# Layer 2 heads reordered in pairs of levels, layer 1 weight folds moved into the layer 0 head norm

## The reference, cut to what matters

```python
q = causal_depthwise_conv(x @ Wq, qcw, qcb); k = ...; v = ...   # 4 taps, then silu
def step(St, inp):
    q_, k_, v_, a_, b_ = inp
    sk = einsum('bhij,bhj->bhi', St, k_)
    err = sk - v_
    Sn = a_[..., None, None] * St - b_[..., None, None] * err[..., None] * k_[..., None, :]
    return Sn, einsum('bhij,bhj->bhi', Sn, q_)
o = layernorm(o) * ln_w + ln_b;  o = o * sigmoid(x @ Wg);  return o @ Wo
```

## Time and profile before

| what | value |
|---|---|
| runs | 2279.02 us median of 3 (2278.3 to 2285.44) |
| profiled execution | 2279.3 us |
| its span, first to last instruction | 2277.6 us |
| mean granted clock of TensorE | 0.909 |
| TensorE busy (matmuls) | 1916.4 us, 84% |
| VectorE, ScalarE, GpSimd busy | 1228.4, 836.2, 461.2 us |

### The profile page before, as it was taken

The page is one execution under the profiler, slowest core; times in us unless marked ns, Lnnn a source line. Parts: engine busy times, 40 slices in busy tenths (PEclk is TensorE's granted clock), DMA queues, the critical chain, the costliest instruction groups (busy, mean ns, idle before and its releaser), DMA issues. The chain is left out here.

```text
span 2277.6 us, 52273 instructions
## 1 busy us (share of the span) xinstructions
PE 1916.4 (84%) x21233; PEld 1321.6 (58%) x21233; DVE 1228.4 (54%) x3235; ACT 836.2 (37%) x1973; POOL 461.2 (20%) x536
## 2 busy tenths in 40 slices
PE   7993779997999995765999999999899797679569
PEld 3443644565777562553666766666667684456456
DVE  7957542343663346644566666666666326642641
ACT  1112321221652222223576666666666203220120
POOL 0012410330000332641221221122111003720200
PEclk9996999896999998787999999999999798789779
DMA  5000000621500516751010001001000127830000
GB/s 181 0 1 1 1 1 14 210 94 55 205 1 3 186 38 210 241 208 40 21 41 21 21 22 40 21 21 37 25 22 21 52 46 215 258 149 15 3 2 20
DMA packets 55330, 157.37 MB, mean 69 GB/s; under 512 B 12899, under 2 KB 29881, under 8 KB 50822
## 3 DMA queue, kind: packets, MB, share of 16 engines
q1 hardware_dynamic: 45206, 128.84, 16.9%
q0 software_dynamic: 9888, 25.20, 3.3%
HBM read 115.36 MB, written 40.48 MB: 68 GB/s over the span
## 5 line engine op out<-in xcount | busy, mean ns | idle before, releaser
L2268 PE MATMUL l_heads_ps_p<-xnT,l2a_w 128*128 128x512 f32 x512 | 257.0, 628 | 8.2 <-DMA l2a_w<-in_l_w_heads 8.2
L2668 DVE SCALAR_TENSOR_TENSOR l_heads_taps<-l_heads_padded,l_heads_conv,l_heads_taps 128x1024 f32<-128x1024 f32 x144 | 183.8, 1286 | 8.2 <-ACT l_heads_taps L2494 7.5
L2268 PEld LDWEIGHTS l_heads_ps_p<-xnT,l2a_w 128*128 128x128 f32 x512 | 89.5, 194 | 80.4 <-issue 64.2
L2843 POOL TENSOR_TENSOR l_heads_e<-l2a_table,l_heads_row 128x512 f32<-128x512 f32 x32 | 33.3, 1042 | 390.6 <-DVE l_heads_first L2679 385.3
L198 PE MATMUL norm_turn<-zeros,ident 128*128 128x512 f32 x120 | 67.1, 716 | 53.5 <-PEq L60 53.5
L189 ACT ACT_TABLE_LOAD x10 | 12.8, 1283 | 207.2 <-PEq L60 207.2
L198 PEld LDWEIGHTS norm_turn<-zeros,ident 128*128 128x128 f32 x120 | 26.5, 230 | 88.2 <-issue 88.2
L2493 ACT COPY l_heads_padded<-l_heads_ps_p 128x512 f32<-128x512 f32 x96 | 56.5, 589 | 54.1 <-PE l_heads_ps_p L2268 54.1
L2494 ACT ACTIVATE l_heads_taps<-l_heads_ps_p,l_heads_conv 128x512 f32<-128x512 f32 x96 | 76.0, 792 | 0.0
L1877 ACT ACTIVATE l_heads_e<-l_heads_logit,l_heads_shift 128x128 f32<-128x128 f32 (+1 forms) x128 | 56.6, 443 | 44.5 <-DVE l_heads_shift L1909 44.4
L384 PE MATMUL l_ffn_a_ps_w<-l_ffn_a_term,ident 128*128 128x512 f32 (+1 forms) x180 | 59.9, 479 | 8.9 <-DVE l_ffn_a_term L487 8.9
(11 more groups left out here) (706 smaller groups left out, 4907.6 us busy)
## 6 DMA issues: line engine op xcount, KB each, us to landing
l_results<-zeros SPq DMA_DIRECT2D x24, 512.0 KB, 5.8
l_ffn_a_w_in<-in_l_in_w SPq DMA_DIRECT2D x8, 1536.0 KB, 10.1
l_ffn_b_w_in<-in_l_in_w SPq DMA_DIRECT2D x8, 1536.0 KB, 10.4
l2a_w<-in_l_w_heads SPq DMA_DIRECT2D x16, 512.0 KB, 3.7
l_heads_row<-l_rows SPq DMA_DIRECT2D x16, 512.0 KB, 4.6
l_ffn_a_w_out<-in_l_out_w SPq DMA_DIRECT2D x8, 768.0 KB, 9.1
l_ffn_a_w_in<-l_results SPq DMA_DIRECT2D x8, 768.0 KB, 7.0
l_ffn_b_w_out<-in_l_out_w SPq DMA_DIRECT2D x8, 768.0 KB, 8.8
```

Of the source, the lines that this page charges most:

```text
L2268: mm = pe.matmul(ps_p[half][:], w[b][:, which, c, :], core.xnT[:, c, half * HALF:(half + 1) * HALF], start=(c == 0), stop=(c == KC - 1))
L2668: dve.scalar_tensor_tensor(out=taps[which][:], in0=padded[which][:, :, j:j + SEQ], scalar=conv[p % 2][:, which, j:j + 1], in1=taps[which][ ...
L2843: pool.tensor_tensor(m[:], a, b, ALU.subtract).then_inc(gap_ready, 1)
```

## The change

In `l2_heads_stage` the order on TensorE, ScalarE and VectorE is written anew. `project` is split so that a half can be given in two pieces of one matmul. TensorE's loop:

```diff
                 level(1, 0, h)
+                level(1, 1, h)
                 query_key(0, h)
-                level(1, 1, h)
                 query_key(1, h)
                 level(2, 0, h)
+                level(2, 1, h)
                 if more:
                     project(p, K, "k", 0)
-                level(2, 1, h)
+                turn_keys(h)
+                level(3, 0, h)
+                level(3, 1, h)
                 if more:
                     project(p, K, "k", 1)
-                level(3, 0, h)
-                turn_keys(h)
-                level(3, 1, h)
+                turn_values(1, h)
+                level(4, 0, h)
+                level(4, 1, h)
                 if more:
                     project(p, Q, "q", 0)
-                level(4, 0, h)
                 turn_values(0, h)
-                level(4, 1, h)
-                turn_values(1, h)
                 last_update(0, h)
+                last_update(1, h)
                 if h >= 1:
                     turn_o(h - 1, 0)
-                last_update(1, h)
                 if more:
                     project(p, Q, "q", 1)
                 inner_w(0, h)
                 inner_w(1, h)
-                if h >= 1:
-                    turn_o(h - 1, 1)
                 if more:
                     project(p, V, "v", 0)
                 inner_x(0, h)
                 inner_x(1, h)
+                if h >= 1:
+                    turn_o(h - 1, 1)
                 if more:
-                    project(p, V, "v", 1)
+                    project(p, G, "g", 0)
                 outer_w(0, h)
                 outer_w(1, h)
                 if more:
-                    project(p, G, "g", 0)
+                    project_from(p, V, "v", 1, 0)
                 corner(0, h)
                 corner(1, h)
                 if more:
+                    project_from(p, V, "v", 1, 1)
                     key_key(0, p)
...
                     turn_first(0, p)
-                    project(p, G, "g", 1)
+                    project_from(p, G, "g", 1, 0)
...
                 multiply("b11", "u", h, lambda s: Y[1][:, s, :], lambda s: r[:, s, :])
                 if more:
+                    project_from(p, G, "g", 1, 1)
                     turn_first(1, p)
```

```diff
                 level(2, 1, h)
                 if late:
                     convolve(h, V, 2)
+                    moments(h - 1)
...
                 take_w("w32", 1, h)
                 if more:
+                    convolve(p, K, 1)
                     convolve(p, K, 2)
+                    convolve(p, Q, 0)
```

The folds of layer 1 leave `l1_latent_stage`, with GpSimd's preparation and the copies, and go into `l0_head_norm_stage`, on GpSimd and TensorE beside VectorE's chain. ScalarE's copies stand between its steps of the norm:

```diff
                 act.activation(sd[s][:], spread[s][:], ACT.Sqrt, bias=core.norm_eps[:],
                                scale=1.0 / HEAD).then_inc(sd_ready, 1)
+                if s < 3:
+                    keep_o(s)
+                if s >= 1:
+                    keep_q(s - 1)
+            keep_q(3)
+            act.wait_ge(bias_folded, 1)
+            for e in range(2):
+                rows = slice(e * LATENT, (e + 1) * LATENT)
+                act.copy(folded.q_bias[rows, :], ps_bias[rows, :, e])
+            keep_o(3)
```

More of the change, by code:

```diff
@@ new lines, in _, with fold_out @@
+        @block.tensor
+        def _(pe):
+            def fold_out(g):
+                bank = (*fold_o, fold_q[0])[g]
+                if g == 3:
+                    pe.wait_ge(q_taken, 1)
+                for i in range(2):
+                    for e in range(2):
+                        h = 2 * (2 * g + i) + e
+                        mm = pe.matmul(bank[e * LATENT:(e + 1) * LATENT, i * D:(i + 1) * D], wt.wv[:, h, :],
+                                       wt.wo[:, h, :], start=True, stop=True)
+                mm.then_inc(o_folded, 1)
+            pe.wait_ge(wt.wo_loaded, 32)
+            for g in range(3):
+                fold_out(g)
+            pe.wait_ge(wk_ready, 1)
+            pe.wait_ge(wt.wq_loaded, 16)
+            for g in range(4):
+                for i in range(2):
+                    p = 2 * g + i
+                    for c in range(KC):
+                        for e in range(2):
+                            h = 2 * p + e
+                            at = (i * KC + c) * P + e * LATENT
+                            mm = pe.matmul(fold_q[g][:, at:at + LATENT], wt.wq[:, h, c * P:(c + 1) * P],
+                                           wk_g[:, h, :], start=True, stop=True)
+                mm.then_inc(q_folded, 1)
+            for p in range(PAIRS1):
+                mm = pe.matmul(ps_bias[:, p, :], wk_g[:, 2 * p:2 * p + 2, :].rearrange("p e n -> p (e n)"),
+                               wt.columns[:, 0, 2 * p:2 * p + 2], start=True, stop=True)
+            mm.then_inc(bias_folded, 1)
+            fold_out(3)
@@ L1548, in _ @@
             last.then_inc(lat_ready, 1)
-            dve.wait_ge(bias_folded, 1)
-            for e in range(2):
-                rows = slice(e * LATENT, (e + 1) * LATENT)
-                dve.tensor_copy(q_bias[rows, :], ps_bias[rows, :, e])
             dve.wait_ge(turned, 1)
@@ L2614, in _ @@
                 take_level(3, 0, h)
-                if more:
-                    take(p, K, "k", 1)
                 take_level(3, 1, h)
@@ L2632, in _ @@
                     take(p, Q, "q", 1)
+                    take(p, V, "v", 0)
+                take_x(0, h)
+                take_x(1, h)
                 if h >= 1:
@@ L2644, in _ @@
                 take_corner(1, h)
+                if more:
+                    take(p, V, "v", 1)
                 whole("b01", "u", h, u[0])
@@ L2767, in _ @@
                 level(1, 0, h)
+                level(1, 1, h)
                 query_key(0, h)
-                level(1, 1, h)
                 query_key(1, h)
-                if late:
-                    moments(h - 1)
                 level(2, 0, h)
@@ L3816, in build @@
         start_stage(nc, core, t["x"])
+        folding = ctx.enter_context(ExitStack())
+        folded = L1Folded(nc, folding)
         with nc.sbuf_tensor("l0_w", [P, UNITS0, IN0 + D], F32) as w:
```

185 lines of the change are left out of this document (84 added, 101 removed).

## The result

The changed kernel took 2245.07 us in the median of 4 runs (2239.8 to 2253.63), the kernel before 2279.65 us in 4 (2278.3 to 2285.44): a ratio of 0.9846, 95% interval 0.9822 to 0.987, so 1.5% less. The forecast was 2230, its range 2206 to 2260. It was right on the side and 15 us too low.

The account below looks back on a forecast made before the run. TensorE was taken to bound the layer 2 heads and latent stage, VectorE's chain the head norm. 2279.3 less 38 (heads, mostly 2.5 us each) less 11 (folds) gave 2230 us; range 2206 to 2260, the forecast's own range 2214 to 2246.

Parts of the forecast that it names:

- The folds: Folds moved from the latent stage into layer 0's head norm, where TensorE is free: 11 us less (8 to 15).
- The latent stage: Without the folds, this stage ends at 549.4 us instead of 566.1: 16.7 us less.
- the head norm: Stage taking the folds: ScalarE's copies and GpSimd's product hold up its chain, 2.5 us more (1 to 5).
- the layer 1 heads: They start at half clock behind a thin stretch of TensorE work: 2.9 us more (0 to 4).
- The clash of VectorE and GpSimd: In the head norm, GpSimd's 1.90 us product falls on VectorE's first subtraction: up to 1.5 us more.
- fewer alternations: Layer 2 heads: five fewer changes between small and full-array products, 1.0 us less per head (0.4 to 1.4).
- three waits on ScalarE: Layer 2 heads: TensorE's waits for bank p1, the corner and u get covered by other products, 1.8 us less per head.
- new waits on ScalarE: Layer 2 heads: thinner cover of levels, Q half 0, V half 0 and G half 0 wait: 0.8 us more per head.
- issue stalls: Layer 2 heads: TensorE waiting for its own instructions, 0.3 us less of 1.38 per head; can go to 0 or double.
- clock: Layer 2 heads: denser long products between the levels spare some half clock, 0.2 us less per head (0 to 0.45).
- rival 1: The instruction stream limits the dense pairs of levels, idle doubles, a head gains 0.6 us: 2259 us, chance 0.17.
- rival 4: Folds no cheaper where put, head norm bound by ScalarE's copies and layer 1 heads cold: 2241 us, chance 0.07.

Follow-up runs that it names:

- run 1: Each part alone against the kernel before: new order of the layer 2 heads 2259.84 us, moved folds 2267.32 us.
- folds_only: The kernel before with only the folds moved, heads in the old order: 2267.32 us, ratio 0.9925.
- run 2: The changed kernel with SyncE's 1 MB load of a head's weights and decay row held until V half 0 is projected: 2232.4 us, ratio 0.979.
- run 4: The changed kernel with K half 1 between the two chunks of level 3 and Q half 0 between those of level 4: 2241.28 us, ratio 0.9816.
- late_load: Same kernel as run 2, the changed kernel with the 1 MB load held back: 2232.4 us, ratio 0.979.
- split_levels: Same kernel as run 4, the changed kernel with the pairs of levels taken apart: 2241.28 us, ratio 0.9816.
- v0_late: The changed kernel with the 1 MB load held back and ScalarE's scaling of V chunk 0 moved behind the take of Q half 1: 2219.77 us, ratio 0.9716.
- the last run: v0_late with four products of zeros in layer 1's latent stage and the head norm's key weights scaled by ScalarE instead of GpSimd: 2220.87 us, ratio 0.9715.

## Why the prediction was right, and where it was wrong

**The folds, -11 forecast, -12.6 measured.** The latent stage gave 16.6 us (16.7 forecast), the head norm cost 1.9 (2.5) and the layer 1 heads 3.8 (2.9). The clash of VectorE and GpSimd had been put at up to 1.5 us and was 1.6, all on one instruction (the rows it was taken from, differ by 1.49 - 0.41 = 1.08 us, so its size was in part luck), and ScalarE's copies (1.0 forecast) can have cost no more than the 0.3 that is left. The Trainium skill (SBUF — State Buffer, SBUF: two separate sides) says that the two share a pair of ports, held for a whole instruction. The trace agrees in time: VectorE's instruction ended at 186.71, GpSimd's product at 186.65. The three parts add up to -10.9 us. The prediction did not have the clock of other stages. The turn behind the head norm won 1.8 us, the layer 1 projection 1.6, and the end of layer 0's heads and their projection lost some 4. In this execution they nearly cancel, and as run 1 shows, what of it belongs to the folds is open. The rest of the 12.6 lies in other stages, most of it (1.5 us) in the layer 2 experts, which took 147.5 to 152.2 us in the thirteen profiles with no change to their code.

**The heads, -2.5 us each forecast, -1.7 measured.** Term by term, by the two undisturbed heads and the 13:

| term | forecast | measured |
|---|---|---|
| fewer alternations (busy, undisturbed head) | -1.0 | -0.98 |
| three waits on ScalarE | -1.8 | -1.78 |
| new waits on ScalarE | +0.8 | +0.80 |
| issue stalls | -0.3 | +0.28 |
| clock | -0.2 | about 0 |

The new waits even stand where I put them, on `l_heads_shaped` ahead of V half 0 and on the takes. The step that failed is **the instruction stream**. I had read the stalls as a product of dense runs shortly after 1 MB has passed, and had taken 0.3 us off because long products now stand between. The stalls grew from 16.5 to 20.2 us in 13 heads. Other profiles of the same order of heads bear out the direction and show the draw: 17.4 with the old order (`folds_only`), 16.8 to 21.1 with the new one. The longer runs of 256 instructions asked for more, and the load still fell into levels 3 and 4 (run 2, the load held back: 11.1 us less of issue; run 4, the pairs taken apart: 8.6 us less, of the same stalls). The bounds of that term held it ("can go to 0 or double"), the value I took did not. That rival 1 would give 2259 was wrong too: stalls rose by a fifth and did not double.

The clock term, 0.2 forecast, came to nothing: TensorE's busy time fell by 1.00 us a head in the mean and by 0.98 in the undisturbed one. That the denser products between the levels spare half clock is not shown: the 13 heads had 13.7 and 6.8 us of it with the old order (the kernel before, `folds_only`) and 10.2 and 6.8 in the two profiles of the changed kernel. With the load moved there was none, which points to the stalls, but the later versions had some again.

The rest of the gap is the first two head periods. They cost 1.5 us more than before in the profiled execution (39.96 and 44.57 us for 39.17 and 43.90), where I had counted -5. They have 1.6 and 3.2 us on issue. In the second profile of the changed kernel the first of them was 38.11, so part of that is the draw of one execution.

The Trainium skill (Runtime: NRT & Kernel Launch, Instruction fetch mechanics) calls the cost of a crossing "mostly hidden". By count that holds here, since 97 crossings in 13 heads left 18 waits on issue. By time it does not, in so dense a stream: these are 20.2 us, a single stall up to 2.3 us. What it gave as the alternative, no gain from this term, was nearer than mine, though the term cost time.

What held the range: its upper half reached to rival 1 and rival 4, and 2245 lies on the edge of the forecast's own range. Rival 4's number, 2241, came nearer than the forecast, but not by its mechanism: the folds did gain their 11 us and more.

## What to carry to other kernels

Where an engine's instructions are very small, its instruction stream is a resource like a queue. Count them per microsecond in the densest stretch, and keep bulk loads out of that stretch when they have slack. Here one wait on SyncE took 11.6 us off the 13 heads of one profile (medians 13 us apart, with intervals that touch). Before work is moved off a full engine, look at what that engine waits for next. If it only waits longer for the same producer, the late piece is one that stands in the queue behind, and reordering is enough. And when filler or background work leaves a stage, look at the clock of the stages behind it, on both sides of the account.

## What the runs showed of the hardware

- A packet of TensorE's instructions did not start while 1.06 MB of another queue passed (5.1 us with none), and TensorE went on 2.4 us after it came. With the load moved, it came within that stretch. In thirteen traces each stall of 0.5 us or more in the 13 heads ended 2.2 to 3.0 us after a packet's start, and all of TensorE's waits on issue there ended at the same place in 256 instructions (192 to 195 beyond a multiple of 256).
- With the row loaded twice, stalls were 20.3 us in one profile and 25.2 in another, for 19.2 and 20.2 with one load. A late packet costs nothing where TensorE still has work in hand: with the pairs of levels taken apart 11 packets were late behind a load, and one of them cost a stall.
- Two packets never started less than 3.2 us apart in the 13 heads of thirteen traces.
- Half clock in the 13 heads tends to come with the stalls, but is not set by them: 13.7 and 10.2 us in the kernel before and the changed one (issue 16.5 and 20.2), none in `late_load` and `split_levels` (9.1, 11.6), but 3.4 in `v0_late` and 10.2 in the last run, with issue at 11.6 and 11.7.
- One GpSimd product held a VectorE instruction of 0.20 us for 1.83. Sums over the free axis beside GpSimd's small ones took their usual 1.22 us.
- With TensorE's work gone from the latent stage, the layer 1 heads behind it took 3.8 us longer in the changed kernel and 3.5 in `folds_only`, with no change to their code, and 3.1 us less again with products of zeros ahead of them (granted clock 0.97, then 1.00).
